# Five of 32 B products of a Mamba scan taken from GpSimd to TensorE, three C products from VectorE to GpSimd, and the SiLUs of z moved

## The reference, cut to what matters

```python
xi = silu(conv(xi)); dbc = xi @ x_proj.T; dt, Bm, Cm = split(dbc, [64, 80])
dt = softplus(dt @ dt_w.T + dt_b)
dA  = exp(dt[..., None] * A)                      # b, l, 512, 16
dBx = (dt * xi)[..., None] * Bm[:, :, None, :]    # u = dt * xi
h = a * h + bx;  y = einsum('bds,bs->bd', h, c)   # along l, 16 states for each channel
y = (y + xi * D) * silu(z);  out = y @ out_proj.T
```

## Time and profile before

| | |
|---|---|
| median of 3 runs | 4833.41 us (4833.06 to 4835.86) |
| the profiled execution's own time | 4838.41 us |
| its span | 4836.5 us |
| busy over the span: TensorE, VectorE, ScalarE, GpSimd | 89%, 83%, 67%, 72% |
| Mamba layer | about the first 3500 us |
| feed-forward block | the rest |

### The profile page before, as it was taken

The page is one execution under the profiler, slowest core; times in us unless marked ns, Lnnn a source line. Parts: engine busy times, 40 slices in busy tenths (PEclk is TensorE's granted clock), DMA queues, the critical chain, the costliest instruction groups (busy, mean ns, idle before and its releaser), DMA issues. The chain is left out here.

```text
span 4836.5 us, 61589 instructions
## 1 busy us (share of the span) xinstructions
PE 4305.1 (89%) x22500; PEld 3149.4 (65%) x22500; DVE 3992.5 (83%) x4222; ACT 3250.3 (67%) x5217; POOL 3464.0 (72%) x1623
## 2 busy tenths in 40 slices
PE   7888888888888888888888888888799999999999
PEld 3565556556555656665555556555678888888888
DVE  6999999999999999999999999999944444444452
ACT  7777777777777777777777777777444444444443
POOL 5999999999999999999999999999820000000000
PEclk9999999999999999999999999999899999999999
DMA  7433333333333333333333333333230111010100
GB/s 264 140 122 124 114 119 114 107 122 112 127 114 116 116 109 118 117 114 118 111 114 111 110 113 114 112 115 127 93 126 31 35 31 36 31 36 31 35 22 9
DMA packets 176850, 475.34 MB, mean 98 GB/s; under 512 B 15073, under 2 KB 99809, under 8 KB 141921
## 3 DMA queue, kind: packets, MB, share of 16 engines
q1 hardware_dynamic: 175648, 459.83, 28.1%
q10 hardware_dynamic: 896, 11.54, 0.7%
HBM read 435.66 MB, written 47.19 MB: 100 GB/s over the span
## 5 line engine op out<-in xcount | busy, mean ns | idle before, releaser
L1293 DVE TENSOR_TENSOR_SCAN m_h<-bank,m_state,m_dBx 128x512 f32<-128x512 f32 x1792 | 2182.1, 1263 | 35.3 <-ACT bank L1059 29.1
L794 PEld LDWEIGHTS bank<-ident,m_h 128*128 128x128 f32 x8192 | 1009.0, 147 | 655.4 <-issue 335.7
L794 PE MATMUL bank<-ident,m_h 128*128 128x128 f32 x8192 | 1244.5, 283 | 163.0 <-DVE m_h L1302 103.5
L1183 POOL TENSOR_TENSOR m_dBx<-u,m_Bs 128x1024 f32<-128x1024 f32 x512 | 1199.8, 2371 | 2.2 <-issue 0.2
L1183 POOL TENSOR_TENSOR m_dBx<-m_u,m_Bs 128x1024 f32<-128x1024 f32 x512 | 1199.1, 2370 | 2.7 <-DVE m_h L1293 0.6
L1302 DVE TENSOR_TENSOR m_h<-m_h,bank 128x1024 f32<-128x1024 f32 x736 | 880.6, 1197 | 26.0 <-PE bank L776 22.8
L1059 ACT ACTIVATE bank<-m_dt,cols 128x512 f32<-128x512 f32 x1024 | 691.1, 688 | 237.9 <-DVE m_h L1293 234.8
L1059 ACT ACTIVATE bank<-dt,cols 128x512 f32<-128x512 f32 x1024 | 690.7, 688 | 214.7 <-DVE m_h L1293 211.3
L776 PEld LDWEIGHTS bank<-ident,m_Ct 128*128 128x128 f32 x2944 | 345.7, 143 | 678.5 <-DVE m_h L1302 461.4
L776 PE MATMUL bank<-ident,m_Ct 128*128 128x128 f32 x2944 | 486.2, 290 | 315.8 <-DVE m_h L1302 313.1
L296 POOL TENSOR_TENSOR mvj<-mvj,norm_c 128x4 f32<-128x4 f32 x16 | 16.2, 1015 | 984.5 <-DVE mvj L257 984.5
(11 more groups left out here) (165 smaller groups left out, 5206.6 us busy)
## 6 DMA issues: line engine op xcount, KB each, us to landing
m_Bs<-b_dram SPq DMA_DIRECT2D x256, 1024.0 KB, 4.8
m_Cs<-c_dram SPq DMA_DIRECT2D x288, 256.0 KB, 3.2
xx<-in_x SPq DMA_DIRECT2D x16, 512.0 KB, 7.1
xn_dram<-xx SPq DMA_DIRECT2D x16, 512.0 KB, 4.4
yb_dram<-m_ysb SPq DMA_DIRECT2D x16, 512.0 KB, 6.8
xx<-xn_dram SPq DMA_DIRECT2D x16, 512.0 KB, 3.8
x_dram<-m_ysb SPq DMA_DIRECT2D x16, 512.0 KB, 6.8
base<-xn_dram SPq DMA_DIRECT2D x16, 512.0 KB, 3.9
```

The costliest lines, as they stand in the source:

```text
L794: mm = pe.matmul(YB[b][:, o:o + P], h[:, k % NH, m, tok:tok + P], ident[:, :], start=(s == 0 and o == 0), stop=False, is_transpose=True, s ...
L1183: pool.tensor_tensor(dBx[:, k % NDBX, :, :], u[ch.batch][:, m, :], Bs[:, k // BP % 2, k % BP, :].unsqueeze(1).broadcast_to((P, 2, T)), ALU ...
L1293: dve.tensor_tensor_scan(h[:, k % NH, m, flip(ch)], DA[ch.at(STEPS, i) % NDA][:, flip(ch)], dBx[:, k % NDBX, m, flip(ch)], initial, ALU.mu ...
```

## The change

- **Units 19, 22, 25, 28, 31 (A_UNITS).** GpSimd no longer forms their dBx. TensorE turns u of the second half so that tokens lie on partitions (turn_u, two jobs, steps 26 and 29), ScalarE keeps it (keep_uT, steps 29 and 32), scales it per token by B, four 128 x 256 copies for each unit (make_uB, from step 2k - 5 on), and TensorE turns that back into the PSUM bank that had held the decays (fill_a, steps 2k - 2 and 2k - 1). The decays of these tiles go straight to h, and the scan works in place on it.
- **C products.** P_UNITS grows from 9 to 12 units: 18, 20, 24, 26 come in, 25 goes. GpSimd forms 27 dBx and 12 C products for each chunk in place of 32 and 9; VectorE forms 20 C products in place of 23.
- **z's SiLUs** move to steps 24 and 31, right behind xi's.
- **Tables.** out_proj from steps (29, 35) to (32, 38); z's jobs from (50, 52, 54, 56) to (50, 52, 56, 57).
- **Room in SBUF.** ones goes; lng lies over u0 and is loaded in the last chunk. SP's order is fitted to twelve C loads.

```diff
-P_UNITS = (1, 5, 7, 9, 13, 15, 17, 21, 25)
+P_UNITS = (1, 5, 7, 9, 13, 15, 17, 18, 20, 21, 24, 26)
+A_FIRST, A_STEP, NA = 19, 3, 5
+A_UNITS = tuple(A_FIRST + A_STEP * i for i in range(NA))
...
-AT_XI, AT_ZS = (24, 31), (5, 62)
+AT_XI, AT_ZS = (24, 31), (24, 31)
...
+            def fill_a(ch, g):
+
+                for i, k in enumerate(A_UNITS):
+                    m = g - (2 * k - 2)
+                    if not 0 <= m < 2:
+                        continue
+                    tile = ch.at(STEPS, 2 * k + m)
+                    if m == 0:
+                        pe.wait_ge(S["w_made"], ch.at(NA, i + 1))
+                    pe.wait_ge(S["scan"], tile - NDA + 1)
+                    for s in range(TS):
+                        mm = pe.transpose(DA[tile % NDA][:, s * P:(s + 1) * P], uB[:, s, m * P:(m + 1) * P], ident[:, :])
+                    mm.then_inc(S["a_fill"], 1)
...
-                wait(act, S["scan"], ch.at(STEPS, k - NDA + 1))
+                if j in A_UNITS:
+
+                    if m == 0:
+                        act.wait_ge(S["turned"], ch.at(NU, j - NH + 1))
+                    out = h[:, j % NH, m, :]
+                else:
+                    wait(act, S["scan"], ch.at(STEPS, k - NDA + 1))
+                    out = DA[ch.at(STEPS, k) % NDA][:, :]
...
+                    ins = act.activation(uB[:, s, :], uT[:, s, :], ACT.Copy, scale=Ct[:, ch.batch, s, k % DS:k % DS + 1])
...
+                if k in A_UNITS:
+                    dve.wait_ge(S["a_fill"], ch.at(2 * NA, 2 * A_UNITS.index(k) + m + 1))
+                    decays, share = o, da
+                else:
+                    decays, share = da, dBx[:, dbx_ring(ch, k) % NDBX, m, flip(ch)]
+                dve.tensor_tensor_scan(o, decays, share, initial, ALU.mult, ALU.add).then_inc(S["scan"], 1)
```

More of the change, by code:

```diff
@@ L60 @@
 W_LAG, T_LAG = 4, 5
-P_UNITS = (1, 5, 7, 9, 13, 15, 17, 21, 25)
+P_UNITS = (1, 5, 7, 9, 13, 15, 17, 18, 20, 21, 24, 26)
+A_FIRST, A_STEP, NA = 19, 3, 5
+A_UNITS = tuple(A_FIRST + A_STEP * i for i in range(NA))
+B_UNITS = tuple(k for k in range(NU) if k not in A_UNITS)
+NBU = len(B_UNITS)
+W_AHEAD = 5
 D_UNITS = tuple(k for k in range(NU) if k not in P_UNITS)
@@ L470, in weighed, with made, dbx_ring @@
             return sum(j < k for j in (P_UNITS if k in P_UNITS else D_UNITS))
+        def made(k):
+            return sum(j < k for j in B_UNITS) if k >= 0 else sum(j < k + NU for j in B_UNITS) - NBU
+        def dbx_ring(ch, k):
+            return ch.at(NBU, made(k))
         pieces = []
@@ L544, in load_b @@
             def load_b(ch, j):
-                wait(sp, S["dbx"], ch.at(NU, BP * (j - 1)))
+                wait(sp, S["dbx"], ch.at(NBU, made(BP * (j - 1))))
                 if j == 0:
@@ L616, in load_ffn @@
                         sp.dma_start(wm(k, j), a["wmod"][k * P:(k + 1) * P, j * T:(j + 1) * T]).then_inc(S["wm2_in"], 16)
+                for i, name in enumerate(("ln_g", "ln_b", "w3_s")):
+                    sp.dma_start(lng[:, i, :], a[name].partition_broadcast(P)).then_inc(S["lng_in"], 16)
                 J.load_base(sp, (0, 0), xn_v, x_v)
@@ L1090, in body @@
                         evacuate(ch.go(-1), 1)
+                    keep_uT(ch, k)
+                    make_uB(ch, k)
                     if k == EVAC[0]:
@@ L1171, in weigh_b @@
             def weigh_b(ch, k):
+                if k not in B_UNITS:
+                    return
                 half, s = divmod(k, DS)
                 m = slice(2 * half, 2 * half + 2)
-                if k % BP == 0:
+                if k == next(i for i in B_UNITS if i // BP == k // BP):
                     j = k // BP
@@ L1181, in weigh_b @@
                     pool.wait_ge(S["p_ne"], 2 * NPIECE)
-                wait(pool, S["scan"], ch.at(STEPS, 2 * (k - NDBX) + 2))
-                pool.tensor_tensor(dBx[:, k % NDBX, :, :], u[ch.batch][:, m, :],
+                held = unit(ch, B_UNITS[made(k) - NDBX] - (NU if made(k) < NDBX else 0))
+                if held:
+                    pool.wait_ge(S["scan"], held[0].at(STEPS, 2 * held[1] + 2))
+                pool.tensor_tensor(dBx[:, dbx_ring(ch, k) % NDBX, :, :], u[ch.batch][:, m, :],
                                    Bs[:, k // BP % 2, k % BP, :].unsqueeze(1).broadcast_to((P, 2, T)),
@@ L1292, in scan @@
                 initial = 0.0 if ch.opens() else state[:, q, k, m:m + 1]
-                dve.tensor_tensor_scan(h[:, k % NH, m, flip(ch)], DA[ch.at(STEPS, i) % NDA][:, flip(ch)], dBx[:, k % NDBX, m, flip(ch)],
-                                       initial, ALU.mult, ALU.add).then_inc(S["scan"], 1)
+                o, da = h[:, k % NH, m, flip(ch)], DA[ch.at(STEPS, i) % NDA][:, flip(ch)]
+                if k in A_UNITS:
[4 more added lines that the diff above has]
+                dve.tensor_tensor_scan(o, decays, share, initial, ALU.mult, ALU.add).then_inc(S["scan"], 1)
             def weigh_c(ch, k):
```

72 lines of the change are left out of this document (51 added, 21 removed).

## The result

| | before | after |
|---|---|---|
| median of 4 runs each | 4834.64 us (4833.06 to 4836.36) | 4899.56 us (4895.79 to 4903.77) |
| ratio | | 1.0131, 95% interval 1.0119 to 1.0143 |
| span of the profiled execution | 4836.5 us | 4894.0 us |
| end of the Mamba layer's last scan | 3481.5 us | 3539.0 us |

The kernel is 65 us slower. The feed-forward block takes 1355.0 us after the last scan in both, so all of it lies in the Mamba layer. The two profiled executions are 57.5 us apart, 57.6 of it by the last scan.

The account below looks back on a forecast made before the run. VectorE was taken as the bound. 100.7 + 1.43 + 0.8 + 1.7 + 1.9 = 106.5 us a chunk against 105.9, 31 times, less 4 at the ends: +15, 4848 us; own range 4815 to 4880, whole range 4780 to 4905.

Parts of the forecast that it names:

- GpSimd as the bound: Rival: GpSimd's C products of even units wait for states ScalarE saves; 108.0 us a chunk, 4894 us, chance 0.15.
- VectorE's work, 100.7 us: VectorE's own work in a chunk falls from 104.0 to 100.7 us, as three C products leave; A-unit scans cost the same.
- The SiLUs, 1.43 and 0.8 us: Second SiLUs at steps 24 and 31 make scans 25 and 32 wait 1.43 and 0.8 us; scan 63's 0.56 goes.
- The loads: ScalarE's table loads cost 1.30 us each to the next SiLU's start; four fewer free 5.2 us a chunk.
- the rival with that price: ScalarE stands dry behind the load at step 48 for another 1.28 us; 40 us more, 4888 us, chance 0.02.
- TensorE's C waits, both gone: VectorE's waits of 0.47 and 0.38 us a chunk for TensorE's spread C both go.
- The share of step 44, 1.7 us: Scan 44 waits 1.7 us, bounds 1.2 and 2.1, for TensorE's share of unit 22, behind turn_h and a later copy.
- ScalarE from 45 to 55, 1.9 us: Eight scaled copies make ScalarE's stretch 18.3 us against VectorE's 16.4, so it ends 1.9 us late, bounds 1.3 to 3.4.
- The waits add: Over a chunk, VectorE's work and all its new waits add in full: 106.5 us against 105.9.
- the two ends: The last chunk keeps its whole 3.3 us and the prologue saves 1 us at most: 4 us less in all.

Follow-up runs that it names:

- e11: The kernel before with z's SiLUs at steps 24 and 31 in place of 5 and 62, nothing else of the change: 4837.61 us, ratio 1.0004.
- e13: The change with dt's last Exp and Ln at steps 58 and 59 instead of 53 and 54: 4843.92 us, ratio 1.0018.
- e6: The change with 12 of the 20 scaled copies of u a chunk left out, a measurement only: 4821.03 us, ratio 0.9973.
- e7: The change with GpSimd's C products at the nine units of before, so VectorE has three products back: 4911.43 us, ratio 1.0156.
- e1: The change with TensorE issuing the A units' shares (fill_a) ahead of turn_h in their slots: 4873.08 us, ratio 1.0082.

## Why the prediction was right, and where its sizes were off

The direction, the mechanism and the places were right: VectorE stays the pace of a chunk, its work falls, and waits for ScalarE and TensorE take more than it gives. The size was not: +15 us forecast, +65 measured. The forecast gave itself 4815 to 4880 us, and 4899.56 lies outside that; it lies inside the whole range only because that left room for the rival with GpSimd as the bound, which is not what happened. That is luck. Two terms were missed or too small: the wait in slot 29 (19 us) and the full delay at step 44 (13 us).

- **VectorE's work, 100.7 us.** 100.8. The scan of an A unit costs what the others do (1264 and 1262 ns a record), the middle of the bounds.
- **The SiLUs, 1.43 and 0.8 us.** 1.43 and 0.86. Scan 63's 0.56 went, as said. e11 shows that in the kernel before this trade costs nothing, not the 1.2 us a chunk that it counts for in the sum, since a C product's wait of 0.47 goes with it and scan 32 waits 0.53 there.
- **The loads.** The row at 2504.35 has a load of 1.28 us and the decays behind it at 2505.65, 0.02 us after its end. At step 48, the rival's place, the load starts at 2437.23 and dt's Exp at 2438.52, 0.01 us after its end. ScalarE doesn't stand dry behind either, as the trace before said. The Trainium skill (ScalarE: Activation LUTs, What ACT_TABLE_LOAD costs) has a drain beside the load and 2.66 us in all; the trace disagrees again, and the rival with that price is out.
- **TensorE's C waits, both gone.** The 0.47 and 0.38 us did go. This step failed all the same. It laid the 0.38 us to a full C slot, but in the kernel before that product waits in 14 of 32 chunks, and in each of them TensorE had just run at the lower clock (last section). And it looked at the old waits alone. A new one of 1.25 us at slot 29 comes 15 times, 19 us, and e13 and e6 show its cause, the late scan 55.
- **The share of step 44, 1.7 us.** 2.11, the upper bound. The prediction had taken off 0.4 us because out_proj leaves slot 15 free; TensorE's room in slot 15 did not make the dt job earlier. The delay of the dt job by a step of out_proj came in full: TensorE goes on 0.90 us later after scan 42 than before (3.33 against 2.43). 0.41 x 31 = 13 us.
- **ScalarE from 45 to 55, 1.9 us.** 0.53 + 0.23 + 0.13 + 0.91 = 1.80. The copy costs 0.40 to 0.42 us from start to start (2519.84 has the 0.50 us of its record), as taken from between two other sizes. The place was named too, but it was taken as one sum at its end; the waits are spread over four places, and dt's Exp and Ln were among the work that could have been moved. That the size fits so well is in part luck:

```profile
2430.73 0.74 ACT L1105 ACTIVATE m_h<-m_dt,cols 128x512 f32<-128x512 f32 x1
2432.42 0.51 ACT L1120 ACTIVATE m_uB<-m_uT,m_Ct 128x256 f32<-128x256 f32 x1 [0.95 <-PE bank L779]
...
2449.40 0.70 ACT L1105 ACTIVATE bank<-m_dt,cols 128x512 f32<-128x512 f32 x1
```

From the decays of 45 to those of 55 ScalarE takes 18.7 us, 0.95 of them waiting for the late share of step 44, so 17.7 of work, not 18.3. The two new waits are coupled, which the sum didn't have. Nor did the stretch have only 1.5 us to spare before: VectorE then had four C products between scans 44 and 55, not two, so 3.7.
- **GpSimd as the bound.** Three waits of 2.3 us beside the present 1.2 were the rival's price, and the trace has them: 1.16, 1.80, 2.58 and 2.66 us in one chunk, 73.3 us in 1000 against 10.0. But scans wait for a dBx only four times in the layer, 5.7 us, and e7, with GpSimd waiting 124.2 us in 1000, has fewer waits on VectorE. Busy 925 of 1000, it is not the bound. That its time (4894) lies near the measured one is chance.
- **The waits add, the sum says.** They don't quite: e1 takes 1.26 us away and gets 0.42 back.

The bill for the layer: 0.6 us a chunk and -4 were +15 as forecast; +13 for step 44 and +19 for slot 29 make +47. The layer ends 57.6 us later, and the starts of scan 32 in all chunks show why: 31 times 1.1 us (107.0 against 105.9) are 34; slot 29 costs 15 times 1.36 with the lost overlap, 20; one chunk, from the 15th scan 32 to the 16th, takes 116.10 against 111.28, 3.7 more than the others lose, with a scan 6 that waits 3.38 us for TensorE in place of 1.35; and the two ends give back 0.5 us, not 4. The rest up to 65 is how the two profiled executions lie to their medians: that of before above, that of the change below.

## What to carry over

- Ask of work taken off the bound engine where in its order it lies. Ahead of a wait it buys little: in e7 three products more cost 12 us, not 106.
- Cost a block that blocks an in-order engine (a run of copies, two SiLUs between two loads) by its length at that place, not by the engine's average share; then look for what in that stretch can go to another step. e13 moved two entries of a table and gave 56 us.
- Follow a new wait one engine further: what stands idle while it lasts, and what comes right behind it?

## What the runs showed of the hardware that was not expected

TensorE's granted clock fell from 1.00 to 0.50 (1.2 GHz) in 2346 to 2348, though TensorE is busy 88% of the 1000 us around it. Ahead of the fall it had stood 2.10 us. The same 2.10 us in the next chunk left the clock at 1.00, and in the 10 us ahead of the two places TensorE's rows are the same, length for length; what decides between them, no run shows. Over the layer it happened in 15 chunks of 32. With 1.08 us of idleness (e13) no such wait came in the whole layer. Four records of 128 x 512 took 3.03 us instead of 1.88, and VectorE waited 1.25 us for the transposes behind them. An engine off the critical path that is made to stand for 2 us can so come back as a wait on the path.

The kernel before has the same thing in a milder form. Its TensorE ahead of the 0.38 us wait at 2405.89, and the clock:

```profile
2400.85 0.74 PE L794 MATMUL bank<-ident,m_h 128*128 128x128 f32 x4 [1.78 <-DVE m_h L1302]
2401.39 1.92 PE L680 MATMUL bank<-hT,w_in 128*128 128x512 f32 x2
```

```profile
2402.00:2404.00 2.00, 2.00 (x7) 1.14 (x6) 2.00 (x2) 1.98 (x3) 2.00 (x2) 0.50 0.94 389
```

There the two records of a job take 1.92 us in place of 1.02. That product waits in 14 of 32 chunks, and in all 14 a stretch at 0.50 lies in the 6 us ahead of it; of the 18 others 13 have none. So the effect alone doesn't make the change slower: the mean granted clock even rose, from 0.96 to 0.98 in the 1000 us of the earlier trace rows. What counts is whether VectorE needs something from TensorE right behind the fall.
